# Second mixture of experts of a decoder: tile loop unrolled, tokens read in place, one-hots in five operations, output additions in two groups

## The reference

```python
def _moe_linear(x, router_w, expert_w):
    logits = x @ router_w.T
    vals, idx = jax.lax.top_k(logits, K)                     # K = 2
    probs = jax.nn.softmax(vals, axis=-1)
    onehot = jax.nn.one_hot(idx, n_exp, dtype=x.dtype)       # n_exp = 8
    combine = jnp.einsum('tk,tke->te', probs, onehot)
    out = jnp.zeros((x.shape[0], expert_w.shape[1]), x.dtype)
    for e in range(n_exp):
        out = out + combine[:, e:e + 1] * (x @ expert_w[e].T)
    return out
g = _moe_linear(xt, router_gate, w_gate)        # 128 -> 512
u = _moe_linear(xt, router_up, w_up)            # 128 -> 512
inter = jax.nn.silu(g) * u
d = _moe_linear(inter, router_down, w_down)     # 512 -> 128
x = x + d                                       # x was layer-normed to give xt
```

## Time and profile before

| | |
|---|---|
| median of 3 runs | 2872.03 us (2870.92 to 2873.43) |
| profiled execution, its own time | 2873.83 us |
| its span, first to last instruction | 2872.1 us |
| busy in the span: PE, DVE, ACT, POOL | 2436.8, 2139.0, 1537.2, 317.9 us |
| instructions executed; packets of instructions fetched, on two queues | 35,432; 75 + 53, 1.23 + 0.43 MB |
| mean granted TensorE clock | 0.904 of full |
| the last stage, from its first issue of a transfer | 2634.55 us to the end |

### The profile page before, as it was taken

The page is one execution under the profiler, slowest core; times in us unless marked ns, Lnnn a source line. Parts: engine busy times, 40 slices in busy tenths (PEclk is TensorE's granted clock), DMA queues, the critical chain, the costliest instruction groups (busy, mean ns, idle before and its releaser), DMA issues. The chain is left out here.

```text
span 2872.1 us, 35432 instructions
## 1 busy us (share of the span) xinstructions
PE 2436.8 (85%) x10348; PEld 899.4 (31%) x10348; DVE 2139.0 (74%) x3175; ACT 1537.2 (54%) x1850; POOL 317.9 (11%) x332
## 2 busy tenths in 40 slices
PE   5888735899999978999457479999999999995997
PEld 3555401222222123444112213333333333332443
DVE  6877748999998014444487689999999999966665
ACT  4544436577677963333333467666676666652111
POOL 5655510000000000000045000000000000000000
PEclk8987855899999989999679669999999999997999
DMA  3433389100000117776100512013013110112000
GB/s 106 135 121 116 121 137 120 28 26 24 25 24 25 31 29 175 191 191 175 26 0 0 125 51 66 28 41 90 28 31 95 33 30 28 32 34 105 0 0 7
DMA packets 186409, 190.41 MB, mean 66 GB/s; under 512 B 18334, under 2 KB 158307, under 8 KB 184957
## 3 DMA queue, kind: packets, MB, share of 16 engines
q1 hardware_dynamic: 186281, 188.75, 25.9%
HBM read 143.80 MB, written 41.42 MB: 64 GB/s over the span
## 5 line engine op out<-in xcount | busy, mean ns | idle before, releaser
L2423 DVE TENSOR_TENSOR y_acc<-y_acc,y_probs 128x1024 f32<-128x1024 f32 x408 | 496.7, 1217 | 33.9 <-ACT y_probs L2119 23.7
L2119 ACT ACTIVATE y_probs<-y_E,y_mask_bias 128x1024 f32<-128x1024 f32 x416 | 441.0, 1111 | 66.9 <-PE y_E L2204 58.8
L1114 ACT ACTIVATE x_probs<-x_E 128x1024 f32<-128x1024 f32 x408 | 396.8, 1021 | 137.1 <-PE x_E L1160 134.7
L1255 DVE TENSOR_REDUCE x_maxima<-x_M 128x1 f32<-128x496 f32 x676 | 420.5, 668 | 25.5 <-PE x_M L1142 14.1
L2213 PE MATMUL y_O<-y_probs,y_values 128*64 128x512 f32 x1664 | 402.9, 605 | 0.0
L2203 PE MATMUL y_E<-y_qa,y_ks 128*128 128x512 f16 x832 | 319.8, 384 | 1.2 <-ACT y_copied L2095 1.2
L2204 PE MATMUL y_E<-y_qb,y_ks 66*128 66x512 f16 x832 | 318.2, 382 | 0.0
L2095 ACT ACTIVATE y_copied<-y_M 128x1024 bf16<-128x1024 f32 x164 | 167.8, 1023 | 210.9 <-PE y_M L2170 210.9
L2361 DVE TENSOR_REDUCE y_maxima<-y_M 128x2 f32<-128x1024 f32 (+1 forms) x195 | 238.8, 1225 | 36.8 <-PE y_M L2170 25.0
L1576 DVE TENSOR_TENSOR f_hidden<-f_act_out,f_spread 128x512 f32<-128x512 f32 x160 | 110.6, 692 | 169.8 <-ACT f_act_out L1460 162.1
L1160 PE MATMUL x_E<-qs,x_keys 128*128 128x512 bf16 x816 | 220.4, 384 | 4.7 <-ACT x_probs L1114 2.9
(11 more groups left out here) (467 smaller groups left out, 3131.1 us busy)
## 6 DMA issues: line engine op xcount, KB each, us to landing
f_spread<-comb_dram SPq DMA_DIRECT2D x160, 256.0 KB, 3.9
y_values<-v_dram SPq DMA_DIRECT2D x208, 128.0 KB, 2.2
v_dram<-a_v_out SPq DMA_DIRECT2D x26, 512.0 KB, 2.8
k_dram<-a_k_parts SPq DMA_DIRECT2D x26, 512.0 KB, 3.6
x_values<-v_dram SPq DMA_DIRECT2D x100, 128.0 KB, 2.1
f_weights<-f_w_in SPq DMA_DIRECT2D x80, 128.0 KB, 2.4
y_ks<-k_dram SPq DMA_DIRECT2D x75, 128.0 KB, 2.9
v_dram<-a_v_out SPq DMA_DIRECT2D x26, 256.0 KB, 2.0
```

The source lines that it names most:

```text
L1114: nc.scalar.activation(probs[:, n % 2, 2 * g:2 * g + 2, :], psE[:, 2 * g:2 * g + 2, :], ACT.Exp).then_inc(exped, 1)
L1255: V.tensor_reduce(maxima[:, 2 * h + j, qt, c:c + 1], psM[(2 * entry + j) % 3][:, 0:CHUNK0], AX.X, ALU.max).then_inc(max_done, 1)
L2119: A(probs[:, i, :], psE[:, 2 * (i % 2):2 * (i % 2) + 2, :].rearrange("p a b -> p (a b)"), ACT.Exp, bias=mask_bias[:, bass.ds(c * TILES_IN_ ...
L2423: ins = V.tensor_tensor(acc[:, u % 2, :], acc[:, u % 2, :], probs[:, i, :], ALU.add)
```

## The change

The loop over tiles becomes straight code on all three engines, with constant addresses and waits. `xT` is gone; products read their tile's columns of `xnT`, and no product waits for `comb` (product 2 of tile 0 waits for the logits' copy out of bank 2). TensorE waits for `w_down` only ahead of the first down part. The 32 one-hot operations and the sum become two comparisons, two multiplications and a sum over 128x128 elements each, with operands repeated by a zero stride; the down routing keeps its small form. The output additions of a tile become two groups of four (`combine`): group 0 stands between mixing 13 and 14 of the next tile, group 1 after the multiplication one tile later. For the last tile group 1 of tile 6 stands ahead of the multiplication, and both groups of tile 7 at the end. TensorE signals after each down group. TensorE's order of work is unchanged but for tile 0.

```diff
-        def two_largest(V, step, lg, n, out, e, diffed, diffed_at, exped, exped_at):
+        def weights_of_two(V, step, lg, n, e, diffed, diffed_at, exped, exped_at):
...
-            for g in range(n):
-                V.tensor_scalar(one1[:, g, :], iota[:], wheref[:, g, 0:1], p1[:, g:g + 1], ALU.is_equal, ALU.mult)
-                ins = V.tensor_scalar(one2[:, g, :], iota[:], wheref[:, g, 1:2], p2[:, g:g + 1], ALU.is_equal, ALU.mult)
-            step(ins)
-            return V.tensor_tensor(out, one1[:, 0:n, :], one2[:, 0:n, :], ALU.add)
...
-                body(0, True, False)
-                with e.Fori(0, TILES - 1) as t:
-                    body(t + 1, False, False)
-                body(TILES, False, True)
+                for t in range(TILES):
+                    e.wait_ge(S["mixed"], ITEMS * t + ITEMS - 1)
+                    need(e, S["inter_done"], t)
+                    A(silu[:], gate[1][:], ACT.Silu).then_inc(S["silu_done"], 1)
+                    e.wait_ge(S["i_tr"], t + 1)
+                    need(e, S["down_mm"], 2 * t)
+                    need(e, S["rd_mm"], t)
+                    A(interT[:].rearrange("p c t -> p (c t)"), B[4][:], ACT.Copy).then_inc(S["iT"], 1)
+                    e.wait_ge(S["ddiff"], t + 1)
+                    A(ediff[:, 0:1], diff[:, 0:1], ACT.Exp).then_inc(S["dexp"], 1)
...
-                    for n in items:
-                        e.wait_ge(S["mixed"], t * ITEMS + (n + MIX0 - 3))
-                        T.matmul(B[n % 4][:], xT[:], w_in[:, n // 2, n % 2, :], start=True, stop=True)\
+                    if t == TILES:
+                        return
+                    for n in items:
+                        if (t, n) == (0, 2):
+                            e.wait_ge(S["logits_sb"], 1)
+                        need(e, S["mixed"], ITEMS * t + n - 3)
+                        T.matmul(B[n % 4][:], xnT[:, P * t:P * t + P], w_in[:, n // 2, n % 2, :], start=True, stop=True)\
                             .then_inc(S["in_mm"], 1)
...
+                products(0, range(ITEMS))
+                e.wait_ge(S["w_down_loaded"], 16)
+                for t in range(TILES):
+                    products(t + 1, range(0, 5))
+                    turn(t)
+                    products(t + 1, range(5, 8))
+                    route(t)
+                    down(t, 0)
+                    products(t + 1, range(8, 12))
+                    down(t, 1)
+                    products(t + 1, range(12, ITEMS))
...
+                weights_of_two(V, step, logits, n, e, S["diffed"], 1, S["exped"], 1)
+                by_expert = lambda column: column.to_broadcast([P, n, E1])
+                for one, at in ((one1, 0), (one2, 1)):
+                    ins = V.tensor_tensor(one[:], iota[:].unsqueeze(1).to_broadcast([P, n, E1]),
+                                          by_expert(wheref[:, :, at:at + 1]), ALU.is_equal)
+                step(ins)
+                for one, p in ((one1, p1), (one2, p2)):
+                    ins = V.tensor_tensor(one[:], one[:], by_expert(p[:].unsqueeze(2)), ALU.mult)
+                step(ins)
+                step(V.tensor_tensor(comb[:].rearrange("p (a b) -> p a b", b=E1), one1[:], one2[:], ALU.add))
...
+                def combine(t, g):
+                    e.wait_ge(S["down_mm"], 2 * t + g + 1)
+                    for ex in range(4 * g, 4 * g + 4):
+                        src = B[6 + g][:, D * (ex % 4):D * (ex % 4) + D]
+                        prev = x[:, t, :] if ex == 0 else y[(ex + 1) % 2][:]
+                        out = x[:, t, :] if ex == E1 - 1 else y[ex % 2][:]
+                        ins = V.scalar_tensor_tensor(out, src, comb_d[:, ex:ex + 1], prev, ALU.mult, ALU.add)
...
+                mix(0, range(ITEMS))
+                for t in range(TILES):
+                    mix(t + 1, range(0, 2))
+                    if t == TILES - 1:
+                        combine(t - 1, 1)
+                    multiply(t)
+                    if 0 < t < TILES - 1:
+                        combine(t - 1, 1)
+                    mix(t + 1, range(2, 10))
+                    route(t)
+                    mix(t + 1, range(10, 14))
+                    combine(t, 0)
+                    mix(t + 1, range(14, ITEMS))
+                combine(TILES - 1, 1)
```

More of the change, by code:

```diff
@@ L2622, in _, with turn, route @@
                 ins.then_inc(S["logits_mm"], 1)
-                e.wait_ge(S["logits_sb"], 1)
                 e.wait_ge(S["w_in_loaded"], 16)
-                e.wait_ge(S["w_down_loaded"], 16)
                 def products(t, items):
+                    if t == TILES:
+                        return
                     for n in items:
-                        e.wait_ge(S["mixed"], t * ITEMS + (n + MIX0 - 3))
-                        T.matmul(B[n % 4][:], xT[:], w_in[:, n // 2, n % 2, :], start=True, stop=True)\
+                        if (t, n) == (0, 2):
+                            e.wait_ge(S["logits_sb"], 1)
+                        need(e, S["mixed"], ITEMS * t + n - 3)
+                        T.matmul(B[n % 4][:], xnT[:, P * t:P * t + P], w_in[:, n // 2, n % 2, :], start=True, stop=True)\
                             .then_inc(S["in_mm"], 1)
+                def turn(t):
+                    e.wait_ge(S["inter_done"], t + 1)
+                    need(e, S["iT"], t)
+                    for c in range(IC):
+                        ins = T.transpose(B[4][:, P * c:P * c + P], inter[:, P * c:P * c + P], ident[:])
+                    ins.then_inc(S["i_tr"], 1)
+                def route(t):
+                    e.wait_ge(S["iT"], t + 1)
+                    for c in range(IC):
+                        ins = T.matmul(B[5][:, 0:E1], interT[:, c, :], router_down[:, c, :], start=(c == 0),
+                                       stop=(c == IC - 1))
+                    ins.then_inc(S["rd_mm"], 1)
                 def down(t, g):
-                    if g == 0:
-                        e.wait_ge(S["y_done"], t - 1 + Y0)
+                    e.wait_ge(S["iT"], t + 1)
+                    need(e, S["y_done"], 2 * t + g - 1)
                     for c in range(IC):
@@ L2637, in down @@
                                        start=(c == 0), stop=(c == IC - 1))
[L2638 to L2668, removed]
-                body(TILES, False, True)
+                    ins.then_inc(S["down_mm"], 1)
+                products(0, range(ITEMS))
[9 more added lines that the diff above has]
+                    products(t + 1, range(12, ITEMS))
             @block.vector
@@ L2674, in _ @@
                 step = Steps(e, S["dve"])
-                e.sem_inc(S["mixed"], MIX0)
-                e.sem_inc(S["y_done"], Y0)
                 norm_statistics(nc, step, x, stats, moments, 1e-5, var[:]).then_inc(S["to_pow"], 1)
@@ L2734, in _, with multiply @@
-                body(0, True, False)
-                with e.Fori(0, TILES - 1) as t:
-                    step.loop(t, STEPS_IN_TILE)
-                    body(t + 1, False, False)
-                counted = step.count - before
-                assert counted == STEPS_IN_TILE, counted
-                step.leave(TILES - 1, STEPS_IN_TILE, counted)
-                body(TILES, False, True)
+                def multiply(t):
+                    e.wait_ge(S["silu_done"], t + 1)
+                    e.wait_ge(S["mixed"], ITEMS * t + ITEMS)
+                    need(e, S["i_tr"], t)
+                    V.tensor_tensor(inter[:], silu[:], up[1][:], ALU.mult).then_inc(S["inter_done"], 1)
+                    e.wait_ge(S["inter_done"], t + 1)
@@ new lines, in combine @@
+                def combine(t, g):
[5 more added lines that the diff above has]
+                        ins = V.scalar_tensor_tensor(out, src, comb_d[:, ex:ex + 1], prev, ALU.mult, ALU.add)
+                        if ex % 4 < 3:
+                            step(ins)
+                        else:
+                            ins.then_inc(S["y_done"], 1)
+                            e.wait_ge(S["y_done"], 2 * t + g + 1)
```

79 lines of the change are left out of this document (20 added, 59 removed).

## The result

The changed kernel takes 2851.74 us (median of 4 runs, 2848.13 to 2855.3) against 2872.73 (4 runs beside them): ratio 0.9926, 95% interval 0.9909 to 0.9944, faster by 21.0. Forecast were 2852.5 and a gain of 19.5. The profiled execution has a span of 2851.9 and its own time is 2853.69, so that its span can be set against the 2872.1 of before.

What follows compares the result with a forecast made beforehand. The last stage's chain of waits was taken to bound the kernel. Gains of 11.6 + 0.8 + 6.1 - 0.75 + 0.2 + 1.5 = 19.5 us bring the median from 2872.03 to 2852.5, range 2848.5 to 2859.

Steps and rivals of the forecast that it cites:

- later turns: Six later tile turns fall from 24.60 to 23.58 us, the stall moving from product 4 to product 6: gain 6.1.
- Start: Stage start until the second tile's first product: quicker one-hots and four early products not waiting for `comb`, gain 11.6 us.
- the row of the same size: Pricing of the five one-hot operations from `comb`'s own 0.29 us in the trace, 1.35 us in all.
- the gap of 0.25: In the first tile, mixing 0 was put 0.25 us behind `comb`'s end, at 2654.19.
- the 4.7 that I had read for the clock's rise: At the stage's start, TensorE's clock was taken to rise 4.7 us after the first product, at 2653.3.
- the price list of the additions: Loop-trace prices for VectorE's mixings, multiplication and additions, such as additions 0.384 us apart, used to schedule a later turn.
- 0.74 of loop overhead: Time behind the eight output additions, ahead of mixing 0, in each loop turn; the change was to lose it.
- End: After TensorE's last product: 0.2 us from a shorter wait, 1.5 from four instead of eight additions following the last matmul.
- Low clock longer: Rival at the stage's start: early products bring no early clock rise, 2.6 us more, 2855.1; chance 0.08.
- Waits keep the turn at 24.6: Rival in the later turns: late VectorE operations delay product 6, the 6.1 us is lost, 2858.6; chance 0.10.
- Exposed table load: Rival on ScalarE: table load stays behind `silu`'s wait and costs double, 8.4 us over six turns, 2861; chance 0.05.
- Instruction fetch: Rival in the straight code: engines stall fetching six more tiles' instructions, gain lost or 0.2% slower, 2878; chance 0.03.

Runs made afterwards that it cites:

- e8: The changed kernel measured and profiled once more, unaltered: 2850.6 us (6 runs), ratio 0.9914, stage 208.5 us.
- e3: The changed kernel with the 32 small one-hot operations and the sum as before: 2859.4 us, ratio 0.995.
- e4: The changed kernel with TensorE's first product waiting until `comb` is done, the five one-hot operations kept: 2855.43 us, ratio 0.994.
- e6: The changed kernel with the second group of additions moved from behind the multiplication to between mixing 7 and 8: 2845.48 us, ratio 0.9894.
- e1: The kernel before with only the tile loop written out on all three engines: 2870.47 us against 2873.91, ratio 0.9986.
- e9: The changed kernel with VectorE's tiles 1 to 6 in a two-turn loop, three tiles each, waits and weight addresses by register: 2857.18 us, ratio 0.9937.
- e10: As e9, but a tile's 16 weights are first copied to fixed columns, leaving mixings only waits by register: 2859.16 us, ratio 0.9942.

## Why the prediction was right

The time came out as forecast, its make-up only in part: the later turns gave 4.4 us more than their term, and the medians hide it by chance, since the parts ahead of the stage took longer beside it.

*Start.* Right to 0.1. `comb` ended at 2658.86 less 4.9 = 2653.96, forecast 2653.94: the row of the same size was the right price, and the zero stride costs nothing here (an operation with it takes 0.29, as the sum without it does). Mixing 0 came 0.2 sooner than with the gap of 0.25 that I had put in. The early products' own pace did not matter, since TensorE waited for mixing 0 behind them: they took 5.22 here and 5.94 in e8, and the start is 34.68 and 34.69 to the first tile's transposes. So nothing hangs on the 4.7 that I had read for the clock's rise, which the earlier trace rows put at 4.8. e3 and e4 show both parts of the edit as causes.

*Later turns.* The mechanism was right: one wait, at product 6, behind the second group, and e6 shows by taking it away that nothing else holds the turn. Its size was wrong, 10.5 against 6.1, and the step that failed is the price list of the additions: I took "multiplication to next VectorE operation 0.93, of which 0.25 is the gap that a wait leaves" and "product start to its mixing 1.25" from a loop and used them for straight code. After, the same pieces are 0.71 and 1.06 (2734.30, product 12, to 2735.36), and the gap ahead of mixings 14 and 2 is 0.03 each. The chain from product 13 (2735.16) to product 6 (2744.13) takes 8.97; I had it at 9.79 (from -2.57 to 7.22). The difference of 0.82 explains the 0.73 by which a turn is shorter. e1 found the same saving in the old order (0.89), and e9 gave it back by registers alone (0.78). What I called "0.74 of loop overhead" was seen, but only as a thing at the loop's turn; part of it is register work, and that stands ahead of operations all through the turn.

*End.* 2.8 instead of 1.7 in the first profile, 1.9 in e8. The four additions came as reckoned. The wait was 0.83 shorter in both, not 0.2; the gaps behind additions and mixings, 0.03 instead of 0.25, are the likely reason, since the same pieces lie in it. The rest is the clock: in the first profile the transposes still ran before it fell (0.72 instead of 1.12 before and 1.11 in e8), and in e8 the down matmuls took 0.48 longer than before. That e8 comes so near to 1.7 is luck, two misses against each other.

*The rivals.* *Low clock longer*: not here (clock 0.91 from 2656 to 2658), but e3 shows it behind a pause of 5.75. *Waits keep the turn at 24.6*: no. *Exposed table load*: no; the load starts 8 us ahead of `silu` in each turn, as in the last tile before. The Trainium skill, "ScalarE: Activation LUTs", section "What ACT_TABLE_LOAD costs", adds a drain of 1.38 us to the load at each switch. The trace does not agree: in a turn of the kernel before, `silu` at 2749.99 starts 0.01 behind the end of its load, and in the rows above a load starts 0.03 behind the exponential ahead of it:

```profile
2748.70 1.28 ACT L2597 ACT_TABLE_LOAD   x1
2749.99 0.63 ACT L2597 ACTIVATE g_silu<-g_gate 128x512 f32<-128x512 f32 x1
```

*Instruction fetch*: no. From 2700 to 2830 the kernel before fetched no packet and the changed one five; TensorE's only waits there are those at product 6.

## What to carry to other kernels

A gap read in a loop belongs to the loop: before its prices are used for straight code, subtract the register work ahead of waits and operands (0.78 us of a turn of 23.63 in e9, the branch apart). Work that must come between two uses of a bank goes where its engine waits anyway: four additions ahead of mixing 2 cost 0.9 a turn, and ahead of mixing 8 nothing. Measure a stage by its own start and end when its share of the program is small; the stages ahead moved it by up to 9 us between executions.

## What was not expected of the hardware

A wait against a register's value costs VectorE about 0.16 more than one against a constant where the data is there already (0.19 and 0.03) and nothing where VectorE waits anyway (1.06 in both); an operand address from a register costs about 0.1 in either place (0.30, 1.16). The loop's branch is dearer in e9 and e10, with three tiles to a turn, than in the kernel before, with one. In e9 it cost 2.2 (the idle 2.21 above). In the kernel before the whole gap at the turn is 0.74, and with 0.25 to 0.30 of register work taken off, some 0.45 is left, as an estimate. In e9 the instruction packets beside the pause, from 2757 to 2766, are

```profile
q14 instruction: 3, 0.02, 1.1%
```

one each in 2760 to 2762, 2762 to 2764 and 2764 to 2766; the pause is 2760.4 to 2762.6. Inside its turns single packets of this queue fall in 2692 to 2694, 2720 to 2722 and 2752 to 2754 with no pause of VectorE beside them, and from 2700 to 2830 the kernel before fetched none. That agrees with the Trainium skill, "Runtime: NRT & Kernel Launch", section "Instruction fetch mechanics", by which a taken branch to code that is no longer at hand waits for its fetch, while straight code is fetched ahead. No run changed the length of the loop's body by itself, so that this is the cause stays an inference.

Also open is what sets the moment at which TensorE's clock changes. The same kernel behaved differently in two executions: behind the first early product the clock rose after 3 us in the first profile and after 4.5 in e8 (granted 0.61 from 2653 to 2654, 1.00 from 2654 to 2655, first product at 2649.23), and at the end it fell behind the start of the transposes in one and ahead of it in the other. So a difference of this kind between two kernels, each with one profile, shows nothing about their code.
